# ScalarE multiplies by the inverse step in the quantised stage, and the selective scan's side work moves to other iterations

## The reference

```python
def _quant_dequant(v, axis):
    scale = jnp.maximum(jnp.max(jnp.abs(v), axis=axis, keepdims=True) / 127.0, 1e-8)
    return jnp.clip(jnp.round(v / scale), -127.0, 127.0) * scale
gate_up = einsum(xq, w1q)            # 1024 tokens, 256 -> 2 x 704
h = silu(gate) * up
return einsum(hq, w2q)               # 704 -> 256
```

```python
skip, u = xn @ W_skip.T, silu(conv(xn @ W_in.T) + conv_b)
delta = softplus(u @ Wd1.T @ Wd2.T + bd2)
Bt, Ct, A = u @ WB.T, u @ WC.T, -exp(A_log)
h = exp(delta * A) * h + (delta * u) * B     # over the 256 steps of a sequence
y = sum over states of h * C
return ((y + u * W_D) * silu(skip)) @ W_out.T
```

## Time and profile before

| | |
|---|---|
| median of 3 runs | 1730.33 us (1724.32 to 1738.72) |
| profiled execution, its own time | 1733.68 us |
| its span on the core | 1732.4 us |
| busy share of the span | PE 88%, DVE 70%, ACT 50%, POOL 20% |
| quantised stage | about 1134 to 1205 us of the span |
| selective stage | about 1205 to 1493 us, its loop from 1250.74 us |

### The profile page before, as it was taken

The page is one execution under the profiler, slowest core; times in us unless marked ns, Lnnn a source line. Parts: engine busy times, 40 slices in busy tenths (PEclk is TensorE's granted clock), DMA queues, the critical chain, the costliest instruction groups (busy, mean ns, idle before and its releaser), DMA issues. The chain is left out here.

```text
span 1732.4 us, 16497 instructions
## 1 busy us (share of the span) xinstructions
PE 1523.6 (88%) x5247; PEld 833.0 (48%) x5258; DVE 1220.6 (70%) x1989; ACT 873.1 (50%) x1586; POOL 353.8 (20%) x226
## 2 busy tenths in 40 slices
PE   4997789778899999987999999766888888999998
PEld 1565355357644444433555555323333333457776
DVE  7586467345347637768898988577888999756665
ACT  5554254355413213257878888435856544334443
POOL 1000332323001101100000000000177878113331
PEclk8998999998789999999999999875989999999999
DMA  2002675261030000022111211101000000101110
GB/s 83 1 1 82 240 239 179 79 99 24 1 147 0 0 15 0 1 74 80 25 52 48 55 47 43 66 20 53 27 0 1 1 0 0 41 31 52 52 52 25
DMA packets 45851, 88.22 MB, mean 51 GB/s; under 512 B 10082, under 2 KB 27444, under 8 KB 43462
## 3 DMA queue, kind: packets, MB, share of 16 engines
q1 hardware_dynamic: 40678, 61.48, 12.3%
q0 software_dynamic: 5088, 25.69, 4.3%
HBM read 70.49 MB, written 7.22 MB: 45 GB/s over the span
## 5 line engine op out<-in xcount | busy, mean ns | idle before, releaser
L2951 POOL TENSOR_TENSOR s_bu<-s_rep,s_du 128x1024 f32<-128x1024 f32 x64 | 151.0, 2361 | 558.8 <-ACT s_rep L2819 519.3
L2763 DVE TENSOR_TENSOR_SCAN s_bu<-bank,s_bu 128x1024 f32<-128x1024 f32 x64 | 146.2, 2284 | 10.4 <-ACT bank L2835 6.1
L159 PE MATMUL bank<-e_xs,e_wsp 128*128 128x512 f32 x528 | 127.7, 391 | 0.7 <-issue 0.7
L3048 PE MATMUL bank<-s_bu,ident 128*128 128x512 f32 x256 | 127.1, 620 | 0.6 <-DVE s_dl L2719 0.2
L159 PEld LDWEIGHTS bank<-e_xs,e_wsp 128*128 128x128 f32 x528 | 99.0, 188 | 22.8 <-issue 1.9
L2835 ACT ACTIVATE bank<-s_dl,s_an 128x510 f32<-128x510 f32 x128 | 82.6, 684 | 51.4 <-DVE s_bu L2763 51.4
L159 PE MATMUL bank<-r_am,r_b 128*128 128x512 f32 x240 | 106.0, 593 | 1.4 <-DVE r_am L1716 1.4
L1774 ACT ACTIVATE r_sl<-bank 128x512 f32<-128x512 f32 x28 | 16.7, 598 | 133.1 <-PE bank L159 133.0
L3162 DVE TENSOR_TENSOR e_s<-e_s,bank 128x512 f32<-128x512 f32 (+1 forms) x50 | 34.4, 688 | 69.7 <-ACT e_s L3294 69.7
L159 PE MATMUL bank<-conditioned,g_wqk 128*128 128x512 f32 x160 | 79.2, 620 | 4.1 <-ACT g_th L2216 3.8
L1788 POOL TENSOR_TENSOR r_ys<-r_y,r_y 128x512 f32<-128x512 f32 x14 | 21.0, 1500 | 290.7 <-DVE r_y L1728 290.7
(11 more groups left out here) (518 smaller groups left out, 3556.3 us busy)
## 6 DMA issues: line engine op xcount, KB each, us to landing
g_turn<-g_q SPq DMA_DIRECT2D x64, 128.0 KB, 2.3
e_wgu<-in_e_gu SPq DMA_DIRECT2D x22, 256.0 KB, 2.6
b_vw<-b_values SPq DMA_DIRECT2D x48, 64.0 KB, 3.5
e_wd<-in_e_down SPq DMA_DIRECT2D x22, 128.0 KB, 2.6
r_w<-in_r_w SPq DMA_DIRECT2D x3, 896.0 KB, 8.1
g_wqk<-in_g_qk SPq DMA_DIRECT2D x4, 640.0 KB, 3.8
g_wgv<-in_g_gv SPq DMA_DIRECT2D x4, 640.0 KB, 4.1
g_wo<-in_g_wo SPq DMA_DIRECT2D x4, 512.0 KB, 3.5
```

The costliest lines, as they stand in the source:

```text
L159: last = e.matmul(out, lhs, rhs, start=start and n == 0, stop=stop and n == len(pairs) - 1, skip_group_check=True)
L2763: e.tensor_tensor_scan(b, flat(k.pairs[n % 2][:, :, :]), b, 0.0, ALU.mult, ALU.add).then_inc(k["s_scanned"].up(), 1)
L2951: e.tensor_tensor(m.bu[n % m.NBU][:, :, :], m.rep[:, 2 * np:2 * np + 2, :], m.du[:, et, half(h)].unsqueeze(1).to_broadcast([P, 2, HALF]), ...
L3048: summed = e.matmul(banks[6][:, :], k.ident[:, :], m.bu[(n - 1) % m.NBU][:, i, :], start=np == 0 and i == 0, stop=np == m.NP - 1 and i == ...
```

## The change

In the quantised stage `quantise` is cut in three. VectorE keeps the maximum, the step and the inverse (`quantise_inverse`); ScalarE does the multiplication by the inverse and the addition of the rounding constant, in place and in f32, with the inverse as scale and a new constant column as bias; VectorE does the limits later (`quantise_limit`). In a step VectorE now does: hidden inverse (n-4), row inverse (n-1), the three chunks (n-3), hidden limits (n-4), row limits (n-1). ScalarE does: hidden scaling (n-4), row scaling (n-1), Silu (n-3), hidden bytes (n-4), row bytes (n-1).

In the selective stage the product delta * u of half 0 for et = 2 and 3 goes from VectorE ahead of and in the first job to GpSimd at n = 9 and 11. The lists change, the gate parts stand after GpSimd's multiply of the iteration and not before it, TensorE's `raw` stands ahead of the sum, the exponentials of the softplus are all at n = 17 and the logarithm is at n = 19 behind that iteration's decays, the two copies of the late rows go from n = 17 to 13 with their subtractions (13 to 10, 19 to 16), and the projection and the two residual adds of half 0 come one iteration later. The banded attention is the same in both files.

```diff
-def quantise(k, e, st, src, c, done):
+def quantise_inverse(k, e, st, src, c, done):
...
-    e.reciprocal(st[:, 1, c:c + 1], st[:, 0, c:c + 1]).then_inc(k.v_steps.sem, 1)
-    e.wait_ge(k.v_steps.sem, k.v_tick())
-    e.tensor_scalar(src, src, st[:, 1, c:c + 1], ROUND, ALU.mult, ALU.add).then_inc(k.v_steps.sem, 1)
-    e.wait_ge(k.v_steps.sem, k.v_tick())
+    e.reciprocal(st[:, 1, c:c + 1], st[:, 0, c:c + 1]).then_inc(done.up(), 1)
+
+def quantise_limit(k, e, src, done):
     e.tensor_scalar(src, src, ROUND + 127.0, ROUND - 127.0, ALU.min, ALU.max).then_inc(done.up(), 1)
@@ quantised_vector, step n
-            quantise(k, e, m.st, m.tmp[i][:, :], 4 + tt % 4, k["q_hidden"])
+            quantise_inverse(k, e, m.st, m.tmp[i][:, :], 4 + tt % 4, k["q_hidden_inverse"])
+        tt = n - 1
+        if 0 <= tt < TT:
+            e.wait_ge(*k["q_rows_out"].at(tt + 1))
+            quantise_inverse(k, e, m.st, m.xt[tt % 2][:, :], tt % 4, k["q_rows_inverse"])
...
+        tt = n - 4
+        if 0 <= tt < TT:
+            e.wait_ge(*k["q_hidden_scaled"].at(tt + 1))
+            quantise_limit(k, e, m.tmp[tt % 2][:, :], k["q_hidden"])
         tt = n - 1
         if 0 <= tt < TT:
-            e.wait_ge(*k["q_rows_out"].at(tt + 1))
-            quantise(k, e, m.st, m.xt[tt % 2][:, :], tt % 4, k["q_rows_rounded"])
+            e.wait_ge(*k["q_rows_scaled"].at(tt + 1))
+            quantise_limit(k, e, m.xt[tt % 2][:, :], k["q_rows_rounded"])
@@ quantised_scalar, step n
+            x = m.tmp[tt % 2][:, :]
+            e.wait_ge(*k["q_hidden_inverse"].at(tt + 1))
+            e.activation(x, x, ACT.Identity, scale=m.st[:, 1, 4 + tt % 4:5 + tt % 4], bias=k.eps_col(ROUND)).then_inc(k["q_hidden_scaled"].up(), 1)
+        tt = n - 1
+        if 0 <= tt < TT:
+            x = m.xt[tt % 2][:, :]
+            e.wait_ge(*k["q_rows_inverse"].at(tt + 1))
+            e.activation(x, x, ACT.Identity, scale=m.st[:, 1, tt % 4:tt % 4 + 1], bias=k.eps_col(ROUND)).then_inc(k["q_rows_scaled"].up(), 1)
...
@@ Selective
-    SKIP = [5, 7, 16, 19, 33, 35, 49, 52]
-    OUT = [7, 10, 19, 22, 35, 38, 52, 55]
-    GATE = [8, 12, 21, 25, 37, 40, 54, 57]
+    SKIP = [5, 7, 16, 20, 33, 36, 50, 53]
+    OUT = [8, 10, 21, 23, 36, 39, 53, 56]
+    GATE = [8, 12, 22, 26, 38, 41, 54, 57]
-    STEP = [23, 24, 27, 28, 29, 30, 31, 32]
+    STEP = [24, 25, 28, 29, 30, 31, 32, 33]
@@ selective_vector
-    for et in range(1, 3):
-        e.wait_ge(*k["s_delta"].at(et + 1))
-        e.tensor_tensor(m.du[:, et, half(0)], m.dl[:, et, half(0)], m.u[:, et, half(0)], ALU.mult).then_inc(k["s_du"].up(), 1)
+    e.wait_ge(*k["s_delta"].at(2))
+    e.tensor_tensor(m.du[:, 1, half(0)], m.dl[:, 1, half(0)], m.u[:, 1, half(0)], ALU.mult).then_inc(k["s_du"].up(), 1)
...
-        if n == 0:
-            e.wait_ge(*k["s_delta"].at(4))
-            e.tensor_tensor(m.du[:, 3, half(0)], m.dl[:, 3, half(0)], m.u[:, 3, half(0)], ALU.mult).then_inc(k["s_du"].up(), 1)
...
-        if n in (44, 48):
-            selective_add(k, e, 0, (n - 44) // 4)
+        if n in (45, 49):
+            selective_add(k, e, 0, (n - 45) // 4)
@@ selective_scalar
-        if n == 17:
+        if n == 13:
             e.wait_ge(*k["s_late_rest"].at(1))
...
-        if n in (16, 17):
-            softplus_exp(1, 2 * (n - 16))
-            softplus_exp(1, 2 * (n - 16) + 1)
-        if n == 18:
+        if n == 17:
+            for et in range(ET):
+                softplus_exp(1, et)
+        if n == 19:
             softplus_log(1)
@@ selective_pool
-        if n == 13:
+        if n == 10:
             e.wait_ge(*k["s_late_high"].at(1))
...
-        if n == 19:
+        if n == 16:
             e.wait_ge(*k["s_late_middle"].at(2))
...
-        if n in m.GATE:
-            gate_part(m.GATE.index(n), True)
-        if n - 1 in m.GATE:
-            gate_part(m.GATE.index(n - 1), False)
+        if n in (9, 11):
+            x = (n - 5) // 2
+            e.wait_ge(*k["s_delta"].at(x + 1))
+            e.tensor_tensor(m.du[:, x, half(0)], m.dl[:, x, half(0)], m.u[:, x, half(0)], ALU.mult).then_inc(k["s_du"].up(), 1)
...
+        if n in m.GATE:
+            gate_part(m.GATE.index(n), True)
+        if n - 1 in m.GATE:
+            gate_part(m.GATE.index(n - 1), False)
@@ selective_tensor
+        if n in m.RAW:
+            (raw(1, et), now between the C rows and the sum; before, after the sum)
-        if 39 <= n < 47:
+        if 40 <= n < 48:
             (projection of half 0)
```

More of the change, by code:

```diff
@@ L23 @@
 SBUF = 229344
-EPS = {2.0 ** -23: 0, 1e-6: 1, 1e-5: 2, 1.0: 3, -ROUND: 4, 2.0 ** -23 * 1e-6: 5}
+EPS = {2.0 ** -23: 0, 1e-6: 1, 1e-5: 2, 1.0: 3, -ROUND: 4, 2.0 ** -23 * 1e-6: 5, ROUND: 6}
 SLOT = (0, 1, 0, 1, 0, 1, 2, 0)
@@ L81, in __init__ @@
         self.vecs = b("vecs", [P, d["vecs"].shape[1]])
-        self.eps = b("eps", [P, 6])
+        self.eps = b("eps", [P, 7])
         self.tf, self.gain = b("tf", [P, NB]), b("gain", [P, NB])
@@ L2566, in quantised_scalar @@
             e.activation(m.tmp[i][:, :], m.g[i][:, 0:I], ACT.Silu).then_inc(k["q_silu"].up(), 1)
+        tt = n - 4
+        if 0 <= tt < TT:
+            e.wait_ge(*k["q_hidden"].at(tt + 1))
+            if tt >= 2:
+                e.wait_ge(*k["q_ht"].at(tt - 1))
+            e.activation(m.hb[tt % 2][:, :], m.tmp[tt % 2][:, :], ACT.Identity, bias=k.eps_col(-ROUND)).then_inc(k["q_hidden_bytes"].up(), 1)
         tt = n - 1
@@ L3039, in selective_tensor @@
             spread_c(n)
+        if n in m.RAW:
+            et = m.RAW.index(n)
+            e.wait_ge(*(k["s_late_positive"].at(et) if et else k["s_skip_out"].at(2)))
+            raw(1, et)
         if n:
@@ L3068, in selective_tensor @@
                     part.then_inc(k["s_skip"].up(), 1)
[L3069 to L3072, removed]
-        if 39 <= n < 47:
-            ct, x = divmod(n - 39, 4)
-            if n == 39:
+        if 40 <= n < 48:
+            ct, x = divmod(n - 40, 4)
+            if n == 40:
                 e.wait_ge(*k["s_skip_out"].at(6))
-            if n == 43:
+            if n == 44:
                 e.wait_ge(*k["s_added"].at(1))
```

## The result

| kernel | median us (lowest to highest, runs) | to the kernel before, 95% interval |
|---|---|---|
| before | 1734.32 (1722.23 to 1738.72, 15) | |
| changed | 1720.26 (1714.62 to 1725.62, 15) | 0.9928 (0.9909 to 0.9946) |
| changed, timed again on the chip of the last runs (before: 1736.12 there, 11 runs) | 1721.36 (1708.58 to 1725.49, 6) | 0.9908 (0.9881 to 0.9935) |

What follows compares the result with a forecast made beforehand. VectorE was taken to bound both stages. Quantised stage 5.7 us plus loop 9.4 gave 15.1 off the profiled 1733.7, so 1718.6; runs' median 3.35 lower gave 1715.2 us, range 1710 to 1720.

Steps and rivals of the forecast that it cites:

- Quantised stage: Two instructions a tile moved from VectorE to ScalarE, hidden there: 5.7 us gained, 4 if hand-offs cost more, at most 6.2.
- Start of the loop: Two products leave VectorE; scan 0 comes 0.6 us earlier, scan 1 waits for GpSimd: 0.4 us gained.
- Jobs 4 to 7: A ring of TensorE's spread, ScalarE's copy and TensorE's sum, untouched by the change; its 1.9 us of stalls stay.
- Jobs 8 to 16: Gate behind GpSimd's multiply returns 2.3 of 4.4 us; TensorE's low clock, at even odds, loses 2.0: 1.3 us gained.
- Jobs 17 to 23: Decays 19 go out before ScalarE's log block, so its stall and what followed vanish: 4.8 us gained.
- 36 to 39: Loop jobs where OUT now comes three iterations after SKIP begins, so the tanh's wait holds up no decays: 3.1 us gained.
- Jobs 24 to 34: GpSimd still has a side operation in twelve jobs running, one later: 0.1 us of 1.6 gained.
- Jobs 40 to 63: No stall to give; an output and an add fall together at n = 49: 0.3 us lost (0 to 0.9).
- B: Quantised stage: scaling gives nothing because VectorE waits for ScalarE at each limit; 9.4 us gained, 1721 us, chance 0.12.
- C: Loop: new waits from saturated GpSimd and TensorE's `raw` lose 4 us; 1720 us, chance 0.15.
- D: Everything goes: no low clock, most of the ring's 1.9 us too, 6.2 in the quantised stage; 1711 us, chance 0.08.
- E: Slower: TensorE stays at 1.2 GHz through the loop, each job costing 1.0 us more; 1770 us, chance 0.03.

Runs made afterwards that it cites:

- e3: Changed kernel with VectorE made to wait for its own reciprocal again; quantised stage 60.93 us, a tile 6.28 us.
- e1: Quantised stage as changed, selective stage as in the kernel before; 1727.28 us, ratio 0.9960 to the kernel before.
- e12: Changed kernel unedited, timed again beside the combined one on the same chip; ratio 0.9908 to the kernel before, 1721.36 us.
- e2: Selective stage as changed, quantised stage as in the kernel before; 1724.63 us, ratio 0.9932 to the kernel before.
- e8: Changed kernel with six more matmuls into a free bank in TensorE's idle times before job 0; scan 0 to scan 40 took 138.69 us.
- e5: Changed kernel with SKIP 36 back at 35 and OUT 36, 39 back at 35, 38; job 36 lost 2.36 us, job 39 0.68.
- e10: Changed kernel with only the logarithm back at n = 18; job 19 lost 0.24 us, scan 0 to scan 40 took 140.69.
- e9: Changed kernel with the logarithm, ScalarE's late-row copies and GpSimd's two subtractions back at their old iterations; job 19 lost 1.28 us.
- e7: Changed kernel with GpSimd's two products of delta * u ahead of its multiply of job 4; scan 0 to scan 40 took 140.77 us.
- e11: Changed kernel with GpSimd's products at n = 4, three more matmuls before job 0 and STEP spread; 1718.58 us, ratio 0.9907 to the kernel before.

## Why the prediction was right

**Which engine, and the sum.** Both stages belong to VectorE: right. The stages gave 14.9, 14.9 and 15.8 us in the three profiles of the changed kernel, for 15.1. That the sum fits so closely is in part luck, as two errors cancel: the quantised stage gave 7.2 for 5.7, above the 6.2 that nothing was to pass, and the loop with its start 7.7, 7.7 and 8.6 for 9.4, in two of three profiles under its range of 8 to 11. Scan 0 to scan 40 took 143.2, 143.2 and 141.5 for 141.

**Quantised stage, 5.7 forecast, 7.2 measured.** The prices held (0.98 and 0.60 for 0.97 and 0.6), and the cover: no wait in the steady tiles. Two terms were off. "Nothing lets it pass 6.2" was wrong. I counted the instructions that left and not the wait of VectorE for its own reciprocal that left with them, 1.8 us by e3. The fill cost 0.74 and not 0.35: the first hidden product comes 9.70 us after the first reduction (8.96 before), VectorE waiting 0.67, 1.49 and 0.79 for ScalarE at the first three rows. The tail cost nothing (9.99 for 9.98), though the last limits waited 1.21. e1's stage is 7.2 us shorter with the scaling on ScalarE, which was idle for half of it. The rule of the Trainium skill ("ScalarE: Activation LUTs", "Rules for kernel authors"), VectorE and not ScalarE for add and mul, spoke against the edit; the runs don't agree with it here.

**Start of the loop, 0.4.** Right in e12: scan 0 comes 0.6 earlier, scan 1 then waits 0.64 for GpSimd, and 0.5 is left. In the other two executions scan 0 came 0.97 earlier and 0.85 was left; why is open.

**Jobs 4 to 7, "nothing changes".** Right in e12 and e2 (2.0), wrong in two executions (3.76), where the clock rose one sum later. The cause given for the 1.9, a ring that the change doesn't touch, was wrong in all: by e8 it is the low clock of the first sums.

**Jobs 8 to 16, 1.3.** 1.3 measured, and that is luck: 1.3 was the middle of 2.3 and 0.3 at even odds. The stalls of 1.0, 0.75 and 0.25 that I counted from GpSimd's list were 1.05, 0.73 and 0.22. The low clock came after 2.00 us of idle time and cost 1.0 (0.81 and 0.22 at jobs 13 and 14), not 2.0, in six of the nine profiles with this list; in e5, e8 and e10 it didn't come, after the same 2.0 us.

**Jobs 17 to 23, 4.8, and 36 to 39, 3.1.** Both right to 0.1. e5 shows the cause of the second; for the first, e9 and e10 show that the shorter queue ahead of the block is needed. I had argued it from the block's new place as well, which carries 0.2, and some 1.9 of it no run brings back.

**Jobs 24 to 34, 0.1.** -0.4: jobs 24 and 25 lose 0.16 and 0.22, which they did not in the kernel before. e1, with the old list, loses 0.20 and 0.23 there and 2.03 in all, so this is not the new list's place; the kernel before came to these jobs behind a larger stall at 22 (1.32; 0.18 in e1).

**Jobs 40 to 63, -0.3.** -0.2, by 0.19 at job 48; -0.6 in e12 and e2, with another 0.36 at job 54.

**The rivals.** B would show VectorE waiting at each limit; it does in four of sixteen. C's new waits came where GpSimd's list is full, and had been counted. Of D the gain in the quantised stage came, and the ring's 1.9 only with e8's added matmuls. E did not happen: the loop's last third is at 1.00.

## What to carry to other kernels

When an instruction leaves an in-order engine, count the wait that it made necessary as well: here that was a quarter of the stage's gain. In a loop with one engine at its limit, side work costs nothing only if the next instruction that the limit needs is not queued behind its wait; count the distance in iterations between what makes a tile and what reads it. Savings that were measured one at a time need not add: e7 and e8 gave 2.5 and 4.5 us, their two edits together (e11, with less filling) 4.7 at most.

## What the runs showed of the hardware

TensorE's granted clock was 0.50 from 1249 to 1260 us of the changed kernel, behind idle times of 2.19 and 1.19 us. It also fell after idle times of 2.0 to 2.5 us inside a loop that otherwise keeps it at 1.00, but not each time: with the same list of jobs 8 to 16 and the same 2.0 us it fell in six of nine profiles. In equal kernels it came back one sum earlier or later (job 5: 0.14 or 1.70 us). So single profiles of equal code differ by 1.8 us to scan 40 (143.23 and 141.45). The start of the quantised stage, behind a stretch in which no run changes an instruction, lay between 1135.8 and 1148.6 us; what moves that I have not looked into.

A VectorE product with both operands in SBUF took 2.83 us beside a GpSimd multiply, 0.69 alone, and ended 0.55 us after that multiply; with an operand in a bank a VectorE product took its usual 1.19 us beside GpSimd (1252.22, beside two multiplies from 1250.16). The changed kernel's VectorE, and GpSimd's multiply:

```profile
1241.78 0.69 DVE L2770 TENSOR_TENSOR s_du<-s_dl,s_u 128x512 f32<-128x512 f32 x1
...
1244.34 2.83 DVE L2772 TENSOR_TENSOR s_du<-s_dl,s_u 128x512 f32<-128x512 f32 x1
```

```profile
1244.04 2.58 POOL L2965 TENSOR_TENSOR s_bu<-s_rep,s_du 128x1024 f32<-128x1024 f32 x1 [510.58 <-ACT s_rep L2833]
```

The Trainium skill, "GPSIMD Engine Reference", section "Specifications", lists contention with VectorE instructions that have two SBUF inputs. The rows agree.
